# Two blurs of a four-layer kernel: half of the exponent products move to GpSimd, with their inverse squares spread by DMA, and VectorE evicts the sums

## The reference

```python
h = relu(einsum('bchw,co->bohw', x, w1) + b1)              # 32 hidden channels
ks = relu(einsum('bohw,o->bhw', h, w2[:, 0]) + b2) * 20 + 1
sigma = ks / 3
wgt = exp(-gauss_kernel / (2 * sigma ** 2))                # 9 x 9 taps for every pixel
wgt = wgt / sum(wgt)
low_freq = sum over u, v of xp[:, :, u:u+64, v:v+64] * wgt[..., u, v]
enhanced = x + low_freq
return (enhanced - mean) / sqrt(var + 1e-05)               # over each image's channel
```

## Time and profile before

| | |
|---|---|
| median of 3 runs | 514.49 us (514.17 to 518.37) |
| the profiled execution | 518.3 us, of which the span of its instructions is 516.5 us |
| PE, DVE, ACT, POOL busy | 431.7, 374.6, 279.2, 57.2 us |
| first blur, from its first matmul to its last `stats` | 211.8 to 336.2 us |
| second blur, likewise | 381.1 to 507.5 us |
| granted TensorE clock, mean of the span | 0.931 |

### The profile page before, as it was taken

One profiled execution on the slowest core, in us unless ns is written; L12 is line 12 of the kernel. 1 busy time (PEld: TensorE's weight loads), 2 busy tenths in 40 slices (PEclk: granted clock), 3 DMA queues, 4 the chain that ended last, 5 costly groups with the idle time before them and its releaser, 6 DMA issues. The chain is left out here.

```text
span 516.5 us, 16761 instructions
## 1 busy us (share of the span) xinstructions
PE 431.7 (84%) x7248; PEld 311.4 (60%) x7248; DVE 374.6 (73%) x563; ACT 279.2 (54%) x382; POOL 57.2 (11%) x76
## 2 busy tenths in 40 slices
...
DMA packets 8088, 9.79 MB, mean 19 GB/s; under 512 B 5391, under 2 KB 6752, under 8 KB 7904
## 3 DMA queue, kind: packets, MB, share of 16 engines
...
q10 hardware_dynamic: 1024, 0.36, 0.4%
...
## 5 line engine op out<-in xcount | busy, mean ns | idle before, releaser
L1110 DVE TENSOR_TENSOR g_wgt<-g_exponents,ps 128x1024 f32<-128x1024 f32 x128 | 150.9, 1206 | 4.4 <-PE ps L955 4.3
L1054 ACT ACTIVATE g_wgt<-g_wgt 128x1024 f32<-128x1024 f32 x128 | 132.4, 1061 | 18.6 <-DVE g_wgt L1110 17.7
L955 PE MATMUL ps<-ident,g_scl 128*128 128x128 f32 x512 | 78.9, 283 | 4.5 <-DVE g_scl L1101 3.6
L970 PE MATMUL ps<-g_wgt,g_xt 128*32 128x64 f32 x4096 | 72.6, 223 | 7.5 <-issue 7.4
L970 PEld LDWEIGHTS ps<-g_wgt,g_xt 128*32 128x32 f32 x4096 | 62.0, 111 | 27.2 <-issue 24.1
L955 PEld LDWEIGHTS ps<-ident,g_scl 128*128 128x128 f32 x512 | 56.3, 139 | 16.0 <-DVE g_scl L1101 4.7
L1038 ACT ACTIVATE g_hid<-ps,vec 128x512 f32<-128x512 f32 x32 | 22.0, 688 | 64.5 <-PE ps L914 64.5
L469 PE MATMUL ps<-conv_img,projblk 128*32 128x512 f32 x256 | 35.4, 673 | 0.0
L1351 PE MATMUL ps<-high,wb 128*128 128x512 f32 x72 | 30.6, 426 | 5.3 <-DVE rest L1380 5.3
L526 ACT ACTIVATE biased<-ps,beta_o 128x512 f32<-128x512 f32 x32 | 23.5, 746 | 13.6 <-PE ps L469 13.5
L1061 ACT COPY g_num<-ps 128x512 f32<-128x512 f32 x32 | 18.5, 578 | 22.0 <-PE ps L970 22.0
...
## 6 DMA issues: line engine op xcount, KB each, us to landing
x<-in_x SPq DMA_DIRECT2D x8, 256.0 KB, 6.9
...
windows<-band SPq DMA_DIRECT2D x4, 256.0 KB, 4.9
...
```

Source lines behind the costliest of these rows:

```text
L955: tr = pe.transpose(ps[:, u % 4, P * k:P * k + P], spread(scl[s][:, k, u:u + 1], [P, P]), ident[:])
L970: mm = pe.matmul(ps[32 * j:32 * j + 32, O_BANK, 64 * cb:64 * cb + 64], xt[(s + t) % 2][:, cb, b, :], wgt[s][b][:, t, cb, :], start=(t == 0 ...
L1054: act.activation(w, w, ACT.Exp).then_inc(weight, 1)
L1110: dve.tensor_tensor(wgt[s][u][:], spread(gband[:].unsqueeze(2), shape), spread(s_in, shape), ALU.mult).then_inc(logit, 1)
```

## The change

In rows 1 to 7 the images 2, 3, 6 and 7 (`BY_POOL`) get their exponents from POOL, the others (`BY_DVE`) from DVE as before; row 0 is DVE's alone. POOL reads their inverse squares from SBUF tiles `s_wide`, 512 columns for an image, where DVE reads the spread in PSUM. For this the square and the reciprocal are taken before the transposition, on 128 x 128 values (`act_square` on ACT, `dve_inverse` on DVE); SP stores the 32 useful partitions in DRAM (four DMAs) and loads each image's 512 values into all 128 partitions (four DMAs of 256 KB). Weights are held in pairs of images, and ACT takes exp of a pair at once (2048 columns). DVE evicts the sums (`dve_num`) in ACT's place. The two halves of `hidden` and of `xt` use two banks and one semaphore step each. The order in each row is written anew, and `enhance` and `stats` of row r run in row r+1. The rows of blocks end one earlier (`RB + 1`).

```diff
-    wgt = [[sb(f"wgt{s}{u}", [P, 2, CB, BLK * BLK]) for u in range(B)] for s in range(2)]
+    wgt = [[sb(f"wgt{s}{k}", [P, 2, 2, CB, BLK * BLK]) for k in range(HALF)] for s in range(2)]
...
+    BY_DVE, BY_POOL = (0, 1, 4, 5), (2, 3, 6, 7)
+    s_wide = [[sb(f"s_wide{s}{j}", [P, CB, BLK * BLK]) for j in range(len(BY_POOL))] for s in range(2)]
...
+        for i, bank in enumerate((MLP_BANK, XT_BANK)):
+            mm = pe.matmul(ps[:, bank, :], w1[:, i, :], pad[:, rows, R:R + W], start=True, stop=True)
+        mm.then_inc(hid_mm, 1)
...
+    def pe_ks_turn(pe, r, s):
+
+        pe.wait_ge(small, 3 * r + 2)
+        pe.transpose(ps[:, MLP_BANK, P:2 * P], srow[s][:], ident[:]).then_inc(ks_turned, 1)
...
+        if do.first:
+            for v in range(4, B):
+                pe_spread(pe, 0, 0, v)
+        if do.lag:
+            pe_blur(pe, r - 1, 1 - s, 1, 0)
+            pe_turn(pe, r - 1, 0)
+        if do.next:
+            pe_ks_turn(pe, r + 1, 1 - s)
+        if do.lag:
+            pe_blur(pe, r - 1, 1 - s, 1, 1)
+        if do.next:
+            pe_spread(pe, r + 1, 1 - s, 0)
+            pe_spread(pe, r + 1, 1 - s, 1)
+        if do.main:
+            pe_xt(pe, r + 1, 1 - s)
+        if do.lag:
+            pe_turn(pe, r - 1, 1)
+        if do.main:
+            pe_blur(pe, r, s, 0, 0)
+        if do.next:
+            pe_spread(pe, r + 1, 1 - s, 2)
+        if do.after_next:
+            pe_hidden(pe, r + 2)
+        if do.main:
+            pe_blur(pe, r, s, 0, 1)
+        if do.lag:
+            pe_low(pe, r - 1)
+        if do.next:
+            pe_spread(pe, r + 1, 1 - s, 3)
+        if do.after_next:
+            pe_ks(pe, r + 2)
...
+    def act_square(act, r):
+
+        act.wait_ge(small, 3 * r + 1)
+        act.activation(ks_sq[:], relu[:], ACT.Square, bias=one[:, 0:1], scale=20.0).then_inc(ks_squared, 1)
...
+        w = wgt[s][pair][:].rearrange("p b t k m -> p (b t k m)")
         act.activation(w, w, ACT.Exp).then_inc(weight, 1)
...
+    def act_row(act, r, s, do):
+        if do.next and not do.first:
+            act_square(act, r + 1)
+        if do.main:
+            act_weight(act, r, s, 0 if do.first else 1)
+        if do.next and do.first:
+            act_square(act, r + 1)
+        if do.main:
+            act_weight(act, r, s, 1 if do.first else 0)
+            act_xt(act, r + 1, 1 - s)
+            act_weight(act, r, s, 2 if do.first else 3)
+        if do.after_next:
+            act_hidden(act, r + 2)
+        if do.main:
+            act_weight(act, r, s, 3 if do.first else 2)
...
+    def dve_inverse(dve, r, s):
+
+        dve.wait_ge(ks_squared, r + 1)
+        if not (isinstance(r, int) and r < 3):
+            dve.wait_ge(s_stored, 64 * (r - 2))
+        dve.reciprocal(srow[s][:], ks_sq[:]).then_inc(small, 1)
...
+    def dve_num(dve, r, i):
+
+        dve.wait_ge(blurred, 2 * r + i + 1)
+        if not is0(r):
+            dve.wait_ge(num_turned, 2 * r + i - 1)
+        dve.tensor_copy(num[i][:], ps[:, O_BANK, :]).then_inc(num_out, 1)
...
+        if do.next:
+            dve_relu(dve, r + 1)
+        if do.main:
+            dve_logit(dve, r, s, 0)
+        if do.next:
+            dve_inverse(dve, r + 1, 1 - s)
+        if do.main:
+            dve_logit(dve, r, s, 1)
+        if do.next:
+            dve_scale(dve, r + 1, 1 - s)
+        dve_mix(dve, r - 1, 0)
+        dve_num(dve, r - 1, 1)
+        if do.main:
+            dve_logit(dve, r, s, 2)
+            dve_logit(dve, r, s, 3)
+        dve_mix(dve, r - 1, 1)
+        if do.main:
+            dve_num(dve, r, 0)
+        dve_enhance(dve, r - 1)
+        dve_stats(dve, r - 1)
...
+    def pool_logit(pool, r, s, j):
+
+        b = BY_POOL[j]
+        if j % 2 == 0:
+            pool.wait_ge(s_in[s][j // 2], 16 * r + 16 * s)
+        if not (isinstance(r, int) and r < 2):
+            pool.wait_ge(blurred, 2 * r + b // 4 - 3)
+        shape = [P, 2, CB, BLK * BLK]
+        pool.tensor_tensor(weights_of(s, b), spread(gband[:].unsqueeze(2), shape),
+                           spread(s_wide[s][j][:].unsqueeze(1), shape), ALU.mult).then_inc(logit_p, 1)
+
+    def pool_row(pool, r, s, do):
+        if do.main and not do.first:
+            for j in range(len(BY_POOL)):
+                pool_logit(pool, r, s, j)
+        if do.next:
+            pool_stage(pool, r + 2, s)
...
+            for r in range(1, RB):
+                sp.wait_ge(small, 3 * r + 2)
+                for k in range(4):
+                    sp.dma_start(s_dram[r, :, P * k:P * k + P], srow[r % 2][32 * k:32 * k + B, :]).then_inc(s_stored, 16)
+                sp.wait_ge(s_stored, 64 * r)
+                for j, b in enumerate(BY_POOL):
+                    if r >= 3:
+                        sp.wait_ge(logit_p, 4 * (r - 3) + j + 1)
+                    row = bass.AP(tensor=s_dram.tensor, offset=(r * B + b) * BANK, ap=[[0, P], [1, BANK]])
+                    sp.dma_start(s_wide[r % 2][j][:].rearrange("p k m -> p (k m)"), row).then_inc(s_in[r % 2][j // 2], 16)
...
+            pe_hidden(pe, 0)
             pe_ks(pe, 0)
+            pe_ks_turn(pe, 0, 0)
+            for v in range(4):
+                pe_spread(pe, 0, 0, v)
+            pe_xt(pe, 0, 0)
+            pe_hidden(pe, 1)
+            pe_ks(pe, 1)
```

More of the change, by code:

```diff
@@ new lines, in dve_row, with pool_stage @@
+        dve_enhance(dve, r - 1)
+        dve_stats(dve, r - 1)
+    def pool_stage(pool, g, s):
+        if not (isinstance(g, int) and g < 2):
+            pool.wait_ge(xt_mm, g - 1)
+        for odd in range(2):
+            cols = pad[:, bass.ds(BLK * g, BLK), BLK * odd:BLK * odd + W]
+            ins = pool.tensor_copy(tile[s][:].rearrange("p (k o) r c -> p o k r c", o=2)[:, odd],
+                                   cols.rearrange("p r (k c) -> p k r c", c=QC))
+        ins.then_inc(staged, 1)
```

274 lines of the change are left out of this document (101 added, 173 removed).

## The result

The changed kernel takes 532.33 us (median of 4 runs, 531.34 to 534.27), against 514.49 for the kernel before on the same chip (3 runs, 514.17 to 518.37; its medians beside the later experiments are 517.0 to 518.5): ratio 1.0328, 95% interval 1.0256 to 1.0399. It is slower; the forecast was 518 with a range from 508 to 532. Some executions of a kernel are slower than the rest of the same kernel by over 1.5%, and these are left out of all medians here. The profiled execution took 531.34 us, its span 529.4, 12.9 more than before.

The account below looks back on a forecast made before the run. PE set the pace before, DVE close behind; afterwards a ring of hand-overs through all rows would. Starts 2 x 4.7, rows -2 x 0.9, ends -3.0 and -1.2 gave +3.4 on 514.5: 518 us, range 508 to 532.

Parts of the forecast that it names:

- The start: From PE's first matmul to `relu(2)` in each blur: 29.0 us against 24.3, so +4.7 in each blur.
- a lower clock in the rows: Granted TensorE clock below 1.00 because PE now pauses: counted at nothing, named as a sign of being wrong.
- The ring of rows: Hand-overs from `relu` to next `relu` through DVE, PE and ACT: 13.3 us a row against 13.48, -0.9 in each blur.
- The end: From `relu(7)` to the last `stats`: 29.7 us, against 32.7 and 30.9 before, so -3.0 and -1.2.
- GpSimd and DMA: POOL's logits and the way over DRAM: cost nothing while in time, with 1.5 us of slack.
- L: Time of one GpSimd logit product of 1024 columns: taken as 1.8 us, up to 2.64.
- D: Way of the inverse over DRAM, four stores then loads: 7.8 us, at most 9.2.
- D + 2L: GpSimd's loop, DRAM way plus two products: with 0.35 added it asks for a row of at least 11.8 us.
- Rival C: GpSimd's weights come too late for ACT's first exp of a row: +13 us, 531; chance .25.
- The port: SBUF port shared by VectorE and GpSimd: DVE's operations in the new rows would pay nothing.
- Rival D: DVE's `inverse` and `stats` locked out by GpSimd's products: 2.1 us a row, +21, 539; chance .07.
- Rival B: Engines' relief shows, the ring closes more loosely: rows between 11.1 and 13.3, at 12.2, time 507; chance .13.

Follow-up runs that it names:

- e1: Changed kernel plus spare transposes of the identity in TensorE's waits at each blur's start; 528.07 us, ratio 1.0207 to the kernel before.
- e4: Changed kernel with `enhance` and `stats` two rows back and, on PE, `ks` right behind the blur, turns later; 524.7 us, ratio 1.0161 to the kernel before.
- e10: e4 plus e1's spare transposes, a new ACT and DVE order in the last row, and e9's move; 513.95 us, ratio 0.993 to the kernel before.
- e3: Changed kernel with GpSimd making its first product of each row twice, five products instead of four; 538.37 us, ratio 1.0432 to the kernel before.
- e9: Changed kernel with PE's eight `xt` transposes ahead of two spreads of the next row; 524.06 us, ratio 1.011 to the kernel before.

## Why the prediction was wrong

**The start: mechanism right, size wrong, and this is the step that failed.** The forecast had +4.7 in each blur by a sum at full clock; e1 shows that sum right to 0.3 us (28.7 and 29.0 for 29.0). It then said that a lower clock in the rows is counted "at nothing, since it stayed 1.00 with DVE and ACT waiting here". That stretch is mostly rows of the kernel before, where TensorE was busy 97% of the time; the start, which the change was to stretch with waits, had no stage of its own and no term for the clock. The clock costs 4.0 and 3.8 us of each start (e1). It cost the old kernel 3.8 us in its second blur too, so the second start grew by 4.6 only. The forecast had taken the first blur's 24.3 for both, and its +4.7 for the second came out right by luck, two costs of the clock cancelling. Start: forecast +9.4, measured +13.0.

**The ring of rows: right in kind, 0.35 us short.** Forecast 13.3, bounds 12.9 to 13.8, measured 13.65. Each step is found at its place, from `relu` at 301.57: inverse 302.95, half blur 304.20, spreads 305.24, `xt` 306.16, copy 307.31, half blur 308.56, second half 311.89, `num` 313.15, `enhance` 313.77, `stats` 314.61, `relu` 315.21. The missing 0.35 comes in small pieces: against the forecast's own times the second half starts 0.12 late, `num` 0.18, `enhance` 0.20, and `stats` 0.34, since it follows `enhance` by 0.84 us and not 0.7. Over ten rows that is 3.5 us; the other 1.4 of the 4.9 by which the rows miss are one longer row in each blur (+0.65 and +1.55) less a first row that is shorter (13.22, twice). e4 confirms the ring itself, with 12.33 for the same work in another order.

**Rows longer than their neighbours: not foreseen.** One row of each blur has 14.30 and 15.20 us. In the timeline of PE, second blur:

```profile
458.56 0.54 PE L974 MATMUL ps<-g_wgt,g_xt 128*32 128x64 f32 x24
460.43 0.77 PE L974 MATMUL ps<-g_wgt,g_xt 128*32 128x64 f32 x40 [1.33 <-issue]
```

TensorE stops for 1.33 us in the middle of 64 matmuls that wait for no other engine. The list of DMA queues has an instruction packet of 16 KB just before it; from 458 to 460.5 us:

```profile
q8 instruction: 1, 0.02, 2.3%
```

This packet started at 458.18 and took 0.93 us, so it had landed 1.32 us before TensorE went on. The same holds elsewhere: the two blurs of the thirteen kernels have 140 stops put down to "issue", and 95 of them, from 0.16 to 2.08 us long, end 1.2 to 1.6 us after such a packet on that queue has landed. With 396 of these packets in 3355 us, about 5% of stops would end so by chance (an estimate from these two numbers). Two stops of 0.16 and 0.17 us end 0.2 us after one. The other 43 are no stops of the queue but waits for ACT's copy of `xt`, which the profile fails to name; they end 0.1 to 0.25 us after it. So it is behind `relu(7)` in the changed kernel, shown with the same step in the loop, where the profile has the name:

```profile
320.88 1.01 ACT L1055 COPY g_xt<-ps 128x1024 f32<-128x1024 f32 x1 [0.32 <-PE ps L945]
322.00 1.10 PE L974 MATMUL ps<-g_wgt,g_xt 128*32 128x64 f32 x64 [0.71 <-issue]
...
308.56 1.10 PE L974 MATMUL ps<-g_wgt,g_xt 128*32 128x64 f32 x64 [0.93 <-ACT g_xt L1055]
```

Without these waits the stops are 0.4 and 1.5 us in the rows of the changed kernel and 0.3 and 1.3 in its ends, none in the rows of before and 4.2 and 1.8 in its ends, up to 4.9 in a blur's rows (e10); in e1's ends, 3.3 and 1.8. The Trainium skill (Runtime: NRT & Kernel Launch, section "Instruction fetch mechanics") says that a jump back to a target outside the window that is held makes the engine wait for its instructions. The trace does not bear out the jump as the reason here: in the changed kernel no such packet comes from 285.1 to 313.99 us, while the second pass of the loop runs; in no kernel does a stop begin between `relu(5)` and `relu(7)`; and many lie in the ends, outside the loop. That TensorE waits for its instructions is thus argued from the times of the packets; no run changes them. In the rows of before as many packets land and none is followed by a stop, and why stays open.

**The end: right.** Forecast 29.7, -3.0 and -1.2; measured 29.0 and 29.7, -3.6 and -1.2.

**GpSimd and DMA: no cost in the rows, right, and partly by luck, since two errors cancel.** L was 2.38 for 1.8, inside its bounds; D was 6.4 for 7.8: the four stores were issued and landed in 2.2 us, where the forecast had 3.65 from a load of 32 KB; the loads took 4.1 to POOL's start, for 0.55 + 3.5. D + 2L is 11.1 for 11.4. Rival C falls in the rows, though its time of 531 is the nearest to the measured one; e3 shows that it would decide at about one product more, and e10 that it decides once the row is under 12.

**The port: right.** Beside GpSimd's products a logit takes 1.20 us (1.21 before), the inverse 0.947 us, as the reciprocal of the earlier trace rows, and `stats` 0.69, as in the earlier trace rows. Rival D fell.

**Rival B fell with the ring**, and what it hoped for is there: PE is busy 57.13 of 68.54 us. It takes e4, e9 and e10 to get at it.

**The sum.** Against a forecast of +3.4 on the span it grew by 12.9: 3.6 of the missed 9.5 us are in the starts, 4.9 in the rows (+3.1 for -1.8), -0.6 in the ends and 1.6 outside the blurs. So the rows missed by more us than the starts; but a row of 13.65 lies inside the bounds that the forecast gave it, while the clock at the start had no term and no bound. The medians are 17.8 apart and the forecast stood on the same 514.5; 12.9 and 17.8 differ because the profiled execution of before lies 3.8 above its median and that of after 1.0 below.
